# A ternary-weight decoder layer on one core: all calls in another sequence, the hidden rounding and a row normalisation on ScalarE, key steps on turned keys

## The reference

```
x = x + attn(layernorm(x))       # 16 heads of 32; rope; keys and values squeezed to 8 and grown to 32,
                                 # then quantised to 8 bits over the whole tensor (its min and max);
                                 # windows of 128 at steps of 64, sigmoid scores / their sum, neighbours
                                 # blended by a linear ramp; @ wo.T
x = x + wkv(w, u, layernorm(x), ctx_2048)   # k = the normalised rows, v = the context
    # per channel, over the 256 tokens:  y = (A p + E v) / (A q + E),  with exponentials of w, u, k
x = x + ffn(layernorm(x))        # bit_linear: activations rounded to 8 bits per row, weights to -1, 0, 1
    # by the mean of |w| over the whole matrix
    # h = silu(bit_linear(x, w_gate)) * bit_linear(x, w_up);  h = rms_norm(h) * ln_weight
    # (2048 wide);  bit_linear(h, w_down)
```

## Time and profile before

| | before |
|---|---|
| median of 3 runs (us) | 1038.88 (1038.7 to 1045.11) |
| time of the profiled execution (us) | 1040.61 |
| its span (us) | 1039.3 |
| instructions | 22269 |
| busy TensorE / weight loads (us) | 873.9 (84%) / 526.6 (51%) |
| busy VectorE (us) | 852.9 (82%) |
| busy ScalarE (us) | 660.2 (64%) |
| busy GpSimd (us) | 456.0 (44%) |
| DMA | 107.18 MB |
| chain that ended last, by engine | PE 33%, ACT 19%, DVE 18%, issue 11%, POOL 7%, DMA 5% |

### The profile page before, as it was taken

The page is one execution under the profiler, slowest core; times in us unless marked ns, Lnnn a source line. Parts: engine busy times, 40 slices in busy tenths (PEclk is TensorE's granted clock), DMA queues, the critical chain, the costliest instruction groups (busy, mean ns, idle before and its releaser), DMA issues.

```text
span 1039.3 us, 22269 instructions
## 1 busy us (share of the span) xinstructions
PE 873.9 (84%) x8460; PEld 526.6 (51%) x8460; DVE 852.9 (82%) x1614; ACT 660.2 (64%) x1162; POOL 456.0 (44%) x494
## 2 busy tenths in 40 slices
PE   6985555858899999999989898989899999997775
PEld 3444334545555555555555555656555555553332
DVE  4766495899898989898989898989898989888954
ACT  0227746265767777676868585858585858594633
POOL 1110213226364646464646363646455454546532
PEclk9986676969999999999999999999999999998987
DMA  9977243110425151514132322324151415142122
GB/s 337 412 245 252 107 160 102 44 64 14 85 77 116 56 109 63 104 68 108 64 88 83 79 92 71 101 56 115 49 123 40 112 41 130 33 92 69 34 72 61
DMA packets 119387, 107.18 MB, mean 103 GB/s; under 512 B 91792, under 2 KB 94720, under 8 KB 118128
## 3 DMA queue, kind: packets, MB, share of 16 engines
q1 hardware_dynamic: 116320, 100.64, 33.7%
q10 hardware_dynamic: 2336, 2.52, 0.8%
q0 software_dynamic: 624, 2.59, 0.7%
HBM read 65.62 MB, written 10.75 MB: 73 GB/s over the span
## 4 chain that ended last, share of the span: by engine, by line
PE 33%; ACT 19%; DVE 18%; issue 11%; POOL 7%; DMA 5%; SPq 1%; DVEq 0%; ACTq 0%; POOLq 0%
PE bank L558 10%; PE bank L666 7%; PE bank L646 6%; PE bank L577 5%; ACT arena L926 4%; POOL sums L1827 4%; DMA wide<-wide 3%; ACT junk L981 2%; ACT junk L986 2%; DVE amax L1449 2%; DVE fs L1493 2%; ACT L930 2%; POOL sums L1864 2%; DVE wide L1339 2%; DVE junk L1484 2%
## 5 line engine op out<-in xcount | busy, mean ns | idle before, releaser
L646 PE MATMUL bank<-w_up_gate,qT 128*128 128x512 bf16 x1024 | 238.0, 383 | 22.7 <-DMA qT<-q_tok 17.9
L1844 POOL TENSOR_TENSOR work<-junk,lnw 128x512 f32<-128x512 f32 x128 | 180.4, 1432 | 156.7 <-DVE junk L1484 134.7
L646 PEld LDWEIGHTS bank<-w_up_gate,qT 128*128 128x128 bf16 x1024 | 98.2, 99 | 136.0 <-DMA qT<-q_tok 19.2
L666 PE MATMUL bank<-w_down,work 128*128 128x512 bf16 x512 | 128.4, 400 | 22.6 <-ACT junk L981 13.3
L558 PE MATMUL bank<-wide,wq_sb 128*128 128x256 f32 x512 | 115.9, 385 | 18.9 <-DVE rows L1383 18.9
L926 ACT ACTIVATE arena<-bank 128x384 f32<-128x384 f32 x256 | 104.8, 497 | 36.8 <-PE bank L577 36.7
L608 PE MATMUL bank<-wo_sb,wide 128*128 128x512 f32 x256 | 117.5, 613 | 2.5 <-DVE wide L1376 2.5
L1484 DVE TENSOR_TENSOR junk<-bank,junk 128x512 f32<-128x512 f32 x128 | 86.4, 684 | 37.5 <-PE bank L646 31.9
L558 PEld LDWEIGHTS bank<-wide,wq_sb 128*128 128x128 f32 x512 | 97.2, 192 | 38.3 <-issue 25.4
L965 ACT ACTIVATE work<-work,fs 128x2048 f32<-128x2048 f32 x32 | 63.8, 1995 | 82.2 <-DVE fs L1506 82.2
L577 PE MATMUL bank<-wide,k_win 32*128 32x128 f32 x1536 | 69.0, 315 | 54.3 <-ACT arena L926 30.9
(11 more groups left out here) (155 smaller groups left out, 1508.5 us busy)
## 6 DMA issues: line engine op xcount, KB each, us to landing
...
```

The lines of the kernel that those rows point to most:

```text
L646: last = te.matmul(bank[4 + k % 4][:, :], qT[:, c, t * P:(t + 1) * P], w_up_gate[:, m, c, cols], start=c == 0, stop=c == NC - 1)
L666: last = te.matmul(bank[6 + t][:, :], hid_T[:, t, c, :], w_down[:, c, :], start=c == 0, stop=c == NI - 1)
L1844: ge.tensor_tensor(hid_w[:, t, cols], hid[:, n % 2, :], lnw[:, cols], op=ALU.mult).then_inc(z_set.sem, 1)
```

## The change

It does the following, and each engine's list is written anew around it:

1. **Hidden rounding on ScalarE.** `hidden_round` of VectorE goes. `scale_hidden` adds MAGIC in its own pass, and a new `round_hidden(f, t)` on ScalarE subtracts it in a second pass of 128x2048 and writes bf16.
2. **Normalisation on ScalarE.** `att_norm` keeps the statistics alone. `att_rstd` on GpSimd makes the offset -mean x rstd in two more instructions of 128x2, and the new `normalise_rows(b)` does the 2 halves on ScalarE as scale and bias.
3. **Key steps on turned keys.** `wkv_keys` turns the plain normalised rows, and a new `key_steps(w)` on VectorE adds the table `steps` times minus max(w, 0) to the turned keys in their banks, 4 instructions of 128x256. GpSimd's two subtractions a batch, `grow_tab` and `w_row` go.
4. **Sequence.** The loops on TensorE, VectorE and GpSimd begin one stage further on; fill and drain are re-ordered, SP's loads too. In the round, `wkv_steps(f)` comes behind `residual(w)` and `att_norm(w)` instead of ahead of them. DOWN's `weight_total` comes behind `weigh_windows(1, 0)`.
5. **Tables.** In batch 0, `log_tables(0, 0)` stands behind the logarithms of blocks 0 and 1, and the order is such that a sum of weights no longer stands between blocks 2 and 3: two loads where there were eight.
6. **Spare products.** The two `spin` calls go from the loop. In the fill 15 groups of 1 to 10 come in, between the scores of batches 0 and 1 above all (3, 2, 5, 4, 6, 7, 8, 9, 10), and in the drain four (3, 11, 10, 1).

```diff
@@ scalar_program
-            se.activation(hid_w[:, t, :], hid_w[:, t, :], ACT.Copy, scale=col[t]["qscale"]).then_inc(h_scaled.sem, 1)
+            se.activation(hid_w[:, t, :], hid_w[:, t, :], ACT.Copy, scale=col[t]["qscale"], bias=MAGIC).then_inc(
+                h_scaled.sem, 1)
+
+        def round_hidden(f, t):
+            se.wait_ge(h_scaled.sem, h_scaled.at(f, t))
+            if f:
+                for k in both:
+                    se.wait_ge(hid_turned[t][k].sem, hid_turned[t][k].at(f - 1))
+            se.activation(hid_q[:, t, :], hid_w[:, t, :], ACT.Copy, bias=-MAGIC).then_inc(h_quant.sem, 1)
+
+        def normalise_rows(b):
+            st, mv, rs = stats["att"]
+            se.wait_ge(x1_moved.sem, x1_moved.at(b))
+            se.wait_ge(x1_bn.sem, x1_bn.at(b))
+            for t in range(NT):
+                se.activation(tok[:, t, :], x_rows[b % 3][:, t, :], ACT.Identity, scale=rs[:, t:t + 1],
+                              bias=x1_off[:, t:t + 1]).then_inc(x1_norm.sem, 1)
@@ scalar_program, loop
-            set_keys(b)
             squares(g, 1, 2)
             squares(g, 1, 3)
+            set_keys(b)
             scale_hidden(g, 0)
+            round_hidden(g, 0)
             scale_tokens(f)
             scale_hidden(g, 1)
+            normalise_rows(w)
+            round_hidden(g, 1)
             silu(f, 0, 0)
@@ vector_program
         def att_norm(b):
             row_stats("att", b, x1_bn, x1_mv)
-            ve.wait_ge(x1_rstd.sem, x1_rstd.at(b))
-            normalise("att", x_rows[b % 3], tok, x1_norm)
+
+        def key_steps(w):
+            ve.wait_ge(key_T.sem, key_T.at(w))
...
+            for c in range(NC):
+                turned = in_bank(2 + c // 2, 2)[:, c % 2, :]
+                ve.scalar_tensor_tensor(turned, steps[:, :], sc["shrink"][:, c:c + 1], turned, op0=ALU.mult,
+                                        op1=ALU.add).then_inc(key_stepped.sem, 1)
@@ vector_program, loop
             wkv_quantise(f)
-            wkv_steps(f)
             residual(w)
-            wkv_round(f)
             att_norm(w)
             hidden_scale(g, 1)
-            hidden_round(g, 0)
+            wkv_steps(f)
+            wkv_round(f)
             hidden(f, 0, 0)
-            hidden_round(g, 1)
             rope(b, 0)
+            hidden(f, 0, 1)
+            key_steps(w)
             rope(b, 1)
-            hidden(f, 0, 1)
@@ pool_program
         def att_rstd(b):
             row_rstd("att", b, x1_mv, x1_var, x1_rstd)
...
+            ge.tensor_tensor(x1_off[:, :], mv[:, :, 0], rs[:, :], op=ALU.mult).then_inc(x1_moved.sem, 1)
...
+            ge.tensor_tensor(x1_off[:, :], zero[:, :], x1_off[:, :], op=ALU.subtract).then_inc(x1_moved.sem, 1)
@@ pool_program, fill
         att_rstd(0)
-        key_steps(0)
-        weight_total(DOWN)
         outputs(0, 0)
         weigh_windows(1, 0)
+        weight_total(DOWN)
+        outputs(0, 1)
         weigh_windows(1, 1)
@@ tensor_program, fill and loop
         scores(1, 0)
+        spin(0, 0, 6)
         scores(1, 1)
+        spin(0, 0, 7)
...
         for i in range(4, B):
             b, w, f, g = i, i - 1, i - 2, i - 3
-            spin(g, 16, 2)
...
             down(g, 0, 0)
-            spin(f, 8, 1)
             scores(b, 1)
@@ vector_program, drain
-            wkv_quantise(15)
+            wkv_round(15)
             hidden_scale(14, 0)
-            wkv_residual(15, 0)
...
             peak(14, 1)
-        wkv_quantise(15)
+        hidden_scale(14, 1)
         wkv_steps(15)
-        wkv_round(15)
...
@@ scalar_program, drain
+            scale_hidden(15, 0)
             silu(15, 1, 1)
...
-        scale_hidden(15, 0)
+        round_hidden(15, 0)
         scale_hidden(15, 1)
+        round_hidden(15, 1)
```

681 lines of the change are left out of this document (346 added, 335 removed).

## The result

The changed kernel takes 1053.22 us (median of 4 runs, 1052.02 to 1055.6) against 1039.04 before: a ratio of 1.011, 95% interval [1.008, 1.014]. It is slower by about 1%, where 1015 was forecast, with 1000 to 1032 as the range. The profiled execution has a span of 1051.9 us against 1039.3.

A forecast was written before the change was run, and what follows sets the result against it. A ring of dependences, with no engine full, was taken to bound the kernel; loop -8.0 and -1.7, fill -7.7, drain -6.8 sum to -24.2 from the profiled 1040.61, 1016.4, less 1.73 for the runs' median: 1015 us, range 1000 to 1032.

The forecast's parts named there:

- What shortens that stretch shortens the round: Loop: VectorE's nearly unbroken 21.15 us from refine to the next residual sets the round; work behind the residual doesn't.
- nothing waits longer: Loop, GpSimd: busy 27.69 of 53.13 us and losing the key steps, it makes no engine wait longer; no cost.
- 0.67 us a round for `wkv_steps`: Loop, VectorE: moving it behind the residual shortens each of 12 rounds by 0.67 us, -8.0 us.
- Rival E: Loop: without spare products TensorE's clock falls once every round, 3.1 us each, +37, giving 1052 us; chance 0.06.
- just fit: Loop, ScalarE: two roundings and the normalisations fit into its waits before the first silu, costed at 0.
- -1.7 for spare products that leave: Loop, TensorE: half of the 3.4 us in half-speed rounds comes back, -1.7 us, bounds 0 and -3.4.
- (a): Fill: six table loads of 1.28 us fewer between scores and first output projection, -7.7 us.
- (b): Fill: a sum of weights of 1908 ns no longer stands ahead of the last reciprocal, -1.9 us.
- (c): Fill: GpSimd's code-change pauses around DOWN's moved reduction; the first counted as added, +5.9 us, bounds 0 and +9.5.
- (e): Fill: spare products' clock gain of up to 3.1 us against queueing ahead of scores up to +4, taken as 0.
- (d): Fill: four ternary conversions run faster without key steps on GpSimd, -4.0 us, bounds 0 and -4.0.
- -6.8: Drain: -4 for work moved behind batch 15's token rounding, -2.8 for hidden scale and rounding at the end.

The follow-up runs named there:

- experiment 7: The kernel before with only wkv_steps moved, behind the first hidden_round: 1032.13 us, ratio 0.991.
- 9: The changed kernel with first_state between windows 1 and 2 and its load ahead of the store: 1030.47 us with the loop orders of before, 1031.94 with the change's.
- 11: The changed kernel with DOWN's reduction, the loop orders, first_state and its load as before the change: 1017.5 us, ratio 0.9779.
- the useless copy: The changed kernel plus a GpSimd copy of 4 columns that nobody reads, between windows 1 and 2: 1029.27 us, ratio 0.9902.
- Experiments 1: The changed kernel with its two calls of spare products put back into the loop: 1054.7 us, ratio 1.0132.
- 12: The kernel of 11 with the two calls of spare products put back into its loop: 1022.77 us, ratio 0.9837.
- experiment 4: The changed kernel with DOWN's last sum, reduction and mean back at their places of before in the fill: 1041.2 us, ratio 0.9994.

## Why the prediction was wrong

**The loop.** The failed step is the sentence "What shortens that stretch shortens the round" together with "nothing waits longer" on GpSimd. The term itself, 0.67 us a round for `wkv_steps`, was right: 8.5 us in experiment 7, and 52.4 a round in 9 to 11. But every instruction of the stretch was priced at its row's length while GpSimd's list beside it was changed. A moved copy of 0.3 us closed the gap in which VectorE's two-input instructions got into SBUF. The shown cost is 53.92 - 52.40 = 1.5 us a plain round, 16.7 in eleven; the changed kernel with the useless copy is 24.0 us shorter by its span, of which 20.5 lie in the eleven rounds (the 3.8 beyond 16.7 are fewer and shorter half-speed pieces) and 3.5 ahead of the queries of batch 4. There the copy hasn't run yet; 3.5 is within what the changed fill varies by. The earlier trace rows showed the same contention, 2.29 against 1.28 us for one conversion, and I used it as a gain in the fill and not as a risk in the loop.

**Rival E** had the right side of zero, 1052, and the place wrong. The clock was 1.00 in the plain rounds, 0.97 in those with a dip and 0.94 in one. Its price, 3.1 us a round in the output projection, never came: that took 7.03 in every loop round but one, 7.49 there.

**ScalarE.** The forecast that its pieces "just fit" held to 0.01 us; with so little room that is partly luck. Key steps on VectorE take 1.65 us a round, 1.6 were forecast.

**The half-speed rounds.** I took -1.7 for spare products that leave; 3 such rounds became 7, 2.7 us more (the eleven rounds beyond 11 x 53.92: 6.2 us, before 3.5 beyond 11 x 53.12). Nearly all of it is the one round of 56.42 (2.5): six dips of 0.5 cost what three of 1.0 did. So a dip did get cheaper without the spare products, as the term assumed, and there were more of them. Experiments 1 and 12 show that the spare products don't prevent them, and the same loop had 3 in experiment 4.

**The fill.** Terms (a) and (b), 9.6 us, came out at 9.4 counted from the first sigmoid, of which 7.1 were left at 114.44. Term (c) was mis-sized: +5.9, bound +9.5, and 12 (medians) to 16 us (traces) measured for the group of calls in experiment 4; experiments 9 and 11, timed side by side, differ by 13.0. The step "the windows 1 to 3 of batch 1 wait for both pauses, of which one was on their way before" was wrong in its second half: before, the first pause was hidden in 23.84 us of waiting for VectorE (experiment 4 shows the same with 26.08), and the second ran beside the work on numerators. Term (e) was 0; the spare products are worth 5 to 8 us there. Without (c) the fill is 8.75 us shorter than before (299.60 against 308.35) where my other terms gave 13.6: the round of batch 3 takes 58.3 us instead of 55.1, which no term had. Term (d) wasn't tested by itself.

**The drain**: -6.8 forecast, -6.4 measured. The match is in part luck: -9.5 behind the last peak of batch 14 and +2.4 ahead of it, for which no term stood; what makes the +2.4 stays open.
